# A Mamba and quantised-FFN block on one core: GpSimd's B products in pairs, one C product moved from VectorE to GpSimd

## The chip, the cores and the metric

One core of a Trainium2 chip runs the whole kernel in one launch. The metric is the device time in microseconds (us) from launch to end. A core has TensorE (PE), VectorE (DVE), ScalarE (ACT) and GpSimd (POOL) for computing and SyncE (SP) for issuing most of the transfers; each runs its own instruction stream in order, and they meet at semaphores.

## What is computed

The input x has 8192 tokens of 512 features. First comes a Mamba layer on a modulated layer norm of x, then a feed-forward layer whose inputs and weights are quantised in blocks of 16 to a four-bit grid. Only the Mamba layer's scan is touched by the change. Cut to what matters:

```python
xz = x @ W_in.T;  xc, z = split(xz)             # 1024 inner channels each
xc = silu(conv(xc));  dbc = xc @ W_xproj.T      # delta's rank 32, B and C: 16 states each
delta = softplus(dlt @ W_dt.T + b_dt)
deltaA  = exp(delta[..., None] * A)             # A < 0, one per channel and state
deltaBx = delta[..., None] * B[:, :, None, :] * xc[..., None]
h = deltaA * h + deltaBx                        # along the tokens
y = einsum("bdn,bn->bd", h, C) + xc * D
y = (y * silu(z)) @ W_out.T
```

## The kernel before, in words

**Chunks and units.** The 8192 tokens are cut into 16 chunks of T = 512. Channels lie on the 128 partitions, in eight blocks; two neighbouring blocks make a pair p (four pairs), and each pair has 16 states n. A *unit* u = 16 p + n is one state of one pair: 64 units per chunk. For a unit, tiles are 128 x 2 x 512: two blocks, 512 tokens.

**What happens to a unit.** (1) GpSimd makes the B product (`times_b`, line 717): `slot[u % 8] = du * b_row`, 1024 elements per partition, where du is delta times xc of the pair and b_row is the state's row of B, broadcast to all partitions by a DMA. (2) ScalarE makes the decays exp(rate * delta) in PSUM (`decays`, line 917), two per unit, in two buffers by the parity of u. (3) VectorE scans each of the two blocks (`scan`, line 1050), from the state that the last chunk left. (4) ScalarE saves the last column as the new state (`save_state`, lines 903 and 906). (5) The scan's result is multiplied by c_row. For the 43 units listed in `DVE_C` VectorE does this itself, in two halves right behind the scan (line 1057); for the other 21 (0, 1, 5, 7, 10, 13, 17, 18, 23, 25, 28, 32, 33, 37, 40, 46, 49, 50, 54, 56, 62) GpSimd does it in one instruction (`times_c`, line 724). (6) TensorE adds the unit's product to y by transposing matmuls (`sum_states`, line 1188) and increments `sum_done`, once per unit; that frees the slot.

**Rings.** There are 8 slots, 4 rows of b_row and 4 rows of c_row. A B product of unit u waits for `sum_done` to say that units up to u - 8 are summed, and for its own row of b_row. A load of b_row for unit u waits until B products up to u - 4 are made (`ub_ready`), one of c_row until the C product of u - 4 is made. Each scan of a unit waits for `ub_ready` to reach u + 1.

**The order of the work.** Every engine goes through positions 0 to 63 of each chunk. At position pos GpSimd makes the B product of unit pos, then the C product of unit pos - 2 (`POOL_LAG`) if it is one of its own, then what `POOL_STEPS` lists: a product du at positions 6, 21, 46 and 60, and four tiny operations of the layer norm (`newton`, lines 673 to 676) at 13. VectorE scans unit pos and makes its C product if it is its own; at some positions it adds a gate of the last pair (`DVE_STEPS`, line 963), in the interval after units 4, 5, 21, 32, 36, 49, 51 and 53. TensorE sums unit pos - 3 (`PE_LAG`) and then does what `PE_STEPS` lists: input projections (line 1111), convolution, the small projections, transposes of y and the output projection (lines 1165 and 1169). These tables were written out by hand. At positions 5 to 7 TensorE has the input projections z6 and z7 and five parts of the output projection of the last chunk; z6 needs a PSUM bank that the softplus of pair 1 frees, which ScalarE does at its position 3 (line 853), after the decays of unit 3. Those need the states of unit 1 saved. At its position 15 ScalarE copies a block of the output projection (`residual`, line 872), and TensorE needs that bank before the sum of unit 8. SyncE issues, at each position, the load of b_row for unit pos + 2, the load of c_row for unit pos + 1, and the transfers of `SP_STEPS`.

In chunk 0 the steps that belong to the chunk before are absent, the output projection among them. After the last scan, near 3522 us, the feed-forward layer runs by tiles of 128 tokens.

The GpSimd loop, before:

```python
wait(pool, S["sum_done"], c.at(UNITS, u - SLOTS + 1))
wait(pool, *ring_loaded(b_loaded, c, u))
...
pool.tensor_tensor(slot[:, u % SLOTS, :, :], du[:, p % 2, :, :],
                   two(b_row[:, u % BC_RING, :]), ALU.mult).then_inc(S["ub_ready"], 1)
```

Of the kernel before, what the change touches and what calls it, by code (L numbers as in the profile page):

```python
# [5 lines left out]
P = 128  # L6
# [3 lines left out]
ALU = mybir.AluOpType  # L10
# [5 lines left out]
T = TILES * P  # L16
SLOTS = 8
BC_RING = 4
WIN_RING = 4
UNITS = 64  # L20
# [70 lines left out]
    61: [("load_win", 12, 1)], 63: [("load_win", 13, 1)],  # L91
}
DVE_C = (
    2, 3, 4, 6, 8, 9, 11, 12, 14, 15, 16, 19, 20, 21, 22, 24, 26, 27, 29, 30, 31, 34, 35, 36, 38, 39, 41, 42, 43, 44,
    45, 47, 48, 51, 52, 53, 55, 57, 58, 59, 60, 61, 63,
)

# [21 lines left out]
def wait(eng, sem, value):  # L119
    if not isinstance(value, int) or value > 0:  # L120
        eng.wait_ge(sem, value)
# [9 lines left out]
def adaln_block(nc, x, w_in, w_conv, w_x, w_dt, b_dt, a_log, d_skip, w_out, w_gate, w_up, w_down, c_vec, w_mod, out):  # L131
# [73 lines left out]
    with keep:  # L205
# [3 lines left out]
        def sem(name, stack=keep):  # L209
            return stack.enter_context(nc.semaphore(name))  # L210
# [31 lines left out]
        with mamba:  # L242
            def sb(name, shape, dt=F32, stack=mamba):
                return stack.enter_context(nc.sbuf_tensor(name, shape, dt))
# [20 lines left out]
            du = sb("du", [P, 2, 2, T])  # L265
            slot = sb("slot", [P, SLOTS, 2, T])
            b_row = sb("b_row", [P, BC_RING, T])
# [62 lines left out]
            with setup:  # L330
# [10 lines left out]
                s = lambda name: sem(f"first_{name}", setup)  # L341
# [128 lines left out]
            b_loaded = [sem(f"b_loaded{i}") for i in range(BC_RING)]  # L470
# [14 lines left out]
            S = {n: sem(n) for n in names}  # L485
# [3 lines left out]
            def exists(c):  # L489
                return c.reg is not None or 0 <= c.off < CH  # L490
# [9 lines left out]
            def steps(table, c, pos):  # L500
                return [(step, arg, c.shift(d)) for step, arg, d in table.get(pos, ())
                        if exists(c.shift(d)) and not after_scans(step, c.shift(d)) and not ahead_of_loop(step, c.shift(d))]
# [26 lines left out]
            def two(row):  # L529
                return row.unsqueeze(1).to_broadcast((P, 2, T))  # L530

            def back(c, v):

                return (v, c) if v >= 0 else (v + UNITS, c.shift(-1))
# [10 lines left out]
            def ring_loaded(sems, c, u):  # L545

                per = UNITS // len(sems)
                return sems[u % len(sems)], c.at(16 * per, 16 * (u // len(sems) + 1))
# [6 lines left out]
            with nc.Block() as block:  # L555
# [101 lines left out]
                def _(pool):  # L657
# [26 lines left out]
                    def prep_close(r):  # L684
                        v = prep_rows(r)[:, 0:prep_width(r)]
                        pool.wait_ge(prep_scales, 5 * r + 5)
                        pool.wait_ge(prep_rounded, r + 1)
                        pool.tensor_tensor(blocks(v), blocks(v), spread(prep_scale[r % 3], prep_width(r) // QB),
                                           ALU.mult).then_inc(prep_quant, 1)
                        if r in POOL_SAVES:  # L690
                            prep_save(pool, r)

                    def prepare():
                        for g in range(LAST):
                            prep_mul(g)
                            if g in WOUT_AT:
                                j = 2 * WOUT_AT.index(g)
                                pool.wait_ge(wout_loaded, 16)
                                pool.wait_ge(mix_row, 1)
                                pool.tensor_tensor(wout[:, j:j + 2, :], wout[:, j:j + 2, :],  # L700
                                                   mix_mag.unsqueeze(1).to_broadcast((P, 2, DM)), ALU.mult).then_inc(wout_done, 1)
                            if g >= 1:
                                prep_close(g - 1)
                        prep_mul(LAST)
# [3 lines left out]
                    def times_b(u, c):  # L708
                        p, n = divmod(u, N)
                        if c.reg is None and c.off == 0 and u in range(0, SLOTS, 2):  # L710
                            g = PREP_RING + u // 2
                            pool.wait_ge(prep_saved[g], 16 * len(PREP[g]))
                        wait(pool, S["sum_done"], c.at(UNITS, u - SLOTS + 1))
                        wait(pool, *ring_loaded(b_loaded, c, u))
                        if n == 0:
                            wait(pool, S["u_ready"], c.at(PAIRS, p + 1))
                        pool.tensor_tensor(slot[:, u % SLOTS, :, :], du[:, p % 2, :, :],  # L717
                                           two(b_row[:, u % BC_RING, :]), ALU.mult).then_inc(S["ub_ready"], 1)

                    def times_c(u, c):  # L720
                        h = slot[:, u % SLOTS, :, :]
                        wait(pool, S["state_saved"], c.at(2 * UNITS, 2 * u + 2))
                        wait(pool, *ring_loaded(c_loaded, c, u))
                        pool.tensor_tensor(h, h, two(c_row[:, u % BC_RING, :]), ALU.mult).then_inc(c_row_used[u % BC_RING], 1)  # L724

                    def body(c):
                        for pos in range(UNITS):
                            if exists(c):
                                times_b(pos, c)
                            v, cc = back(c, pos - POOL_LAG)  # L730
                            if exists(cc) and v not in DVE_C:
                                times_c(v, cc)
                            for step, arg, cc in steps(POOL_STEPS, c, pos):
                                HAVE[step](arg, cc)
                                if cc.reg is None and cc.off == 0 and (step, arg) == ("du", 0):
                                    prep_close(LAST - 1)
                            if c.reg is None and c.off == -1 and pos == PREP_AT:
                                prepare()
                            if c.reg is None and c.off == 0 and pos == 3:
                                prep_close(LAST)  # L740
                            if c.reg is None and c.off == CH and pos == PART_ADD_AT:
                                pool.wait_ge(S["part_out"], TILES)
                                for s in range(TILES):
                                    pool.wait_ge(xr_loaded[s], 16 * CH)
                                    pool.tensor_tensor(xr[:, s, :], xr[:, s, :], win[:, s, :, :].rearrange("p k q -> p (k q)"), ALU.add)
                    pool.memset(state[:, :, :], 0.0).then_inc(S["cleared"], 1)
                    pool.memset(halo[:, :, :], 0.0).then_inc(S["cleared"], 1)
                    pool.wait_ge(S["cleared"], 3)
                    all_chunks(pool, body)

                @block.scalar
# [493 lines left out]
        with ffn:  # L1245
# [33 lines left out]
            s = lambda name: sem(name, ffn)  # L1279
# [114 lines left out]
            S = {n: sem("f_" + n, ffn) for n in names}  # L1394
# [475 lines left out]
```

## Time and profile before

| | us |
|---|---|
| three runs | 5140.60, 5141.44, 5143.02 (median 5141.44) |
| profiled execution: span from its first to its last instruction | 5139.8 |
| Mamba half, to the last scan | about 3522 |
| busy in the span: PE / DVE / ACT / POOL | 4759.9 / 4789.5 / 3336.0 / 3832.3 |

The profiled execution has no time of its own beside its span; the span is 1.6 us below the median of the runs. "Busy" is the time in which an engine's records lie. A record of a TensorE matmul ends where it is modelled to end, and records of neighbouring instructions of an engine overlap a little, so spacing (start to start) prices an instruction better than its record. A value in brackets behind a row of the timeline is the idle time of the engine before it and what ended that. L717 is line 717 of the kernel. "x3" in a timeline is three instructions merged in one row.

### The profile page before, as it was taken

The numbers are of one execution on the slowest core, as the hardware profiler recorded it, in microseconds if no ns is written. First come the engines' busy times: TensorE is split into PE (matmuls) and PEld (weight loads), VectorE is DVE, ScalarE is ACT, GpSimd is POOL, SyncE is SP. The second block draws the span as 40 slices with busy tenths as digits, with TensorE's granted clock in tenths as the row PEclk, the third lists the DMA queues.
The fourth block names the chain that finished last, engine by engine and source line by source line (L and its number), as shares of the span: only waits on it lengthen the run. The fifth ranks groups of instructions, "written<-read, shape, count | busy, mean of one in ns | idle before, by whom it ended". The sixth has DMA issues, their size and how long they took to land. (4 is left out here: it accounts for less than half of the span.)

```text
span 5139.8 us, 67238 instructions
## 1 busy us (share of the span) xinstructions
PE 4759.9 (93%) x21964; PEld 3283.1 (64%) x21964; DVE 4789.5 (93%) x5476; ACT 3336.0 (65%) x7037; POOL 3832.3 (75%) x1722
## 2 busy tenths in 40 slices
PE   8799899998999989999999898967999999999999
PEld 3555555555555555555555555555888888888888
DVE  8999999999999999999999999997888888888887
ACT  3777877777777787777777877765444444444442
POOL 6999999999999999999999999994322322322231
PEclk9899999999999999999999999988999999999999
DMA  7555565655656556566566666554010011001000
GB/s 268 173 198 194 189 204 185 196 195 191 199 188 200 195 186 204 186 198 196 188 199 188 194 199 191 187 172 156 25 38 31 31 34 35 31 31 37 31 31 29
DMA packets 402675, 745.79 MB, mean 145 GB/s; under 512 B 44083, under 2 KB 44211, under 8 KB 402198
## 3 DMA queue, kind: packets, MB, share of 16 engines
q1 hardware_dynamic: 401590, 738.08, 43.7%
q8 instruction: 176, 2.88, 0.2%
q0 software_dynamic: 736, 3.41, 0.2%
q14 instruction: 173, 1.42, 0.1%
HBM read 698.05 MB, written 43.26 MB: 144 GB/s over the span
## 5 line engine op out<-in xcount | busy, mean ns | idle before, releaser
L717 POOL TENSOR_TENSOR slot<-du,b_row 128x1024 f32<-128x1024 f32 x1024 | 2397.9, 2379 | 0.2
L1050 DVE TENSOR_TENSOR_SCAN decays<-decays,state,slot 128x512 f32<-128x512 f32 x1376 | 1686.6, 1270 | 61.6 <-POOL slot L717 50.3
L917 ACT ACTIVATE decays<-delta,rate 128x512 f32<-128x512 f32 x2048 | 1385.0, 687 | 50.6 <-DVE slot L998 2.2
L1111 PE MATMUL work_ps<-h_t,win 128*128 128x512 f32 x2048 | 981.8, 627 | 137.5 <-ACT delta L853 109.1
L1188 PEld LDWEIGHTS y_ps<-ident,slot 128*128 128x128 f32 x8192 | 946.2, 143 | 238.2 <-issue 177.9
L1188 PE MATMUL y_ps<-ident,slot 128*128 128x128 f32 x8192 | 1020.9, 277 | 42.6 <-POOL slot L724 30.7
L1574 POOL TENSOR_TENSOR hq<-hid,qinv 128x1408 f32<-128x1408 f32 x63 | 163.5, 2596 | 1001.7 <-DVE qinv L1600 1001.7
L1057 DVE TENSOR_TENSOR slot<-decays,c_row 128x512 f32<-128x512 f32 x1376 | 870.8, 673 | 0.0
L724 POOL TENSOR_TENSOR slot<-slot,c_row 128x1024 f32<-128x1024 f32 x336 | 797.7, 2374 | 81.8 <-ACT state L906 79.7
L1050 DVE TENSOR_TENSOR_SCAN slot<-decays,state,slot 128x512 f32<-128x512 f32 x672 | 819.0, 1263 | 4.0 <-POOL slot L717 2.2
L1111 PEld LDWEIGHTS work_ps<-h_t,win 128*128 128x128 f32 x2048 | 393.7, 201 | 590.0 <-issue 493.1
L1514 ACT ACTIVATE act_gate<-gate_ps 128x512 f32<-128x512 f32 (+1 forms) x192 | 108.3, 564 | 719.9 <-DVE hid L1645 547.5
L1120 PE MATMUL work_ps<-raw,diag 128*128 128x512 f32 x1024 | 465.8, 597 | 27.8 <-ACT raw L798 14.3
L1165 PE MATMUL work_ps<-wout,xc 128*128 128x512 f32 x960 | 447.9, 596 | 32.4 <-ACT xr L872 22.0
L903 ACT ACTIVATE state<-decays 128x1 f32<-128x1 f32 x1376 | 219.1, 159 | 283.7 <-DVE slot L1057 282.6
L1120 PEld LDWEIGHTS work_ps<-raw,diag 128*128 128x128 f32 x1024 | 185.2, 189 | 242.0 <-issue 221.9
L1165 PEld LDWEIGHTS work_ps<-wout,xc 128*128 128x128 f32 x960 | 168.2, 190 | 203.3 <-issue 167.5
L1725 PE MATMUL gate_ps<-w_gate_hi,hx_hi 128*128 128x512 f32 (+1 forms) x768 | 291.9, 380 | 3.4 <-DVE hx_lo L1666 3.4
L1725 PE MATMUL up_ps<-w_up_hi,hx_hi 128*128 128x512 f32 (+1 forms) x768 | 286.0, 372 | 0.0
L1726 PE MATMUL gate_ps<-w_gate_lo,hx_hi 128*128 128x512 f32 (+1 forms) x768 | 286.0, 372 | 0.0
L1727 PE MATMUL up_ps<-w_up_hi,hx_lo 128*128 128x512 f32 (+1 forms) x768 | 285.9, 372 | 0.0
L1727 PE MATMUL gate_ps<-w_gate_hi,hx_lo 128*128 128x512 f32 (+1 forms) x768 | 285.9, 372 | 0.0
(274 smaller groups left out, 7356.9 us busy)
## 6 DMA issues: line engine op xcount, KB each, us to landing
b_row<-b_c_rows SPq DMA_DIRECT2D x1024, 256.0 KB, 3.9
c_row<-b_c_rows SPq DMA_DIRECT2D x1024, 256.0 KB, 3.8
win<-in_w_in SPq DMA_DIRECT2D x256, 256.0 KB, 4.4
xt<-in_x SPq DMA_DIRECT2D x16, 1024.0 KB, 7.1
xr<-in_x SPq DMA_DIRECT2D x64, 256.0 KB, 4.4
x_after_mamba<-xr SPq DMA_DIRECT2D x64, 256.0 KB, 4.6
xa<-x_after_mamba SPq DMA_DIRECT2D x64, 256.0 KB, 3.0
xres<-x_after_mamba SPq DMA_DIRECT2D x64, 256.0 KB, 2.7
```

Of the source, the lines that this page charges most:

```text
L717: pool.tensor_tensor(slot[:, u % SLOTS, :, :], du[:, p % 2, :, :], two(b_row[:, u % BC_RING, :]), ALU.mult).then_inc(S["ub_ready"], 1)
L724: pool.tensor_tensor(h, h, two(c_row[:, u % BC_RING, :]), ALU.mult).then_inc(c_row_used[u % BC_RING], 1)
L917: act.activation(decay[u % 2][:, i, :], delta[:, p % 2, i, :], ACT.Exp, scale=rate[:, 2 * p + i, n:n + 1]).then_inc(S["decay_ready"], 1)
L1050: dve.tensor_tensor_scan(d if u in DVE_C else h, d, h, state[:, 2 * p + i, n:n + 1], ALU.mult, ALU.add).then_inc(S["scan_done"], 1)
L1057: op = dve.tensor_tensor(slot[:, u % SLOTS, i, :], decay[u % 2][:, i, :], c_row[:, u % BC_RING, :], ALU.mult)
L1111: op = pe.matmul(dst[:, :], win[:, i % WIN_RING, k, :], h_t[:, k, :], start=(k == 0), stop=(k == KT - 1))
L1120: op = pe.matmul(dst[:, :], diag[:, j, k, :], raw[:, j % 2, k:k + T], start=(k == 0), stop=(k == TAPS - 1))
L1165: pe.matmul(work_ps[b][:, :], xc[c.parity][:, j, s * P:(s + 1) * P], wout[:, j, :], start=(j == 0), stop=False)
L1188: op = pe.matmul(y_ps[i][:, s, :], slot[:, u % SLOTS, i, s * P:(s + 1) * P], ident[:, :], is_transpose=True, start=False, stop=(n == N - 1 ...
L1725: pe.matmul(dst, lhs[0], rhs[0], start=first, stop=False)
L1726: pe.matmul(dst, lhs[0], rhs[1], start=False, stop=False)
L1727: return pe.matmul(dst, lhs[1], rhs[0], start=False, stop=last)
```

## The change

A B product is made at even units only, for units u and u + 1 in one instruction of 2048 elements per partition. It waits until units up to u - 7 are summed and until both rows of b_row are loaded, and increments `ub_ready` by two when it is done. GpSimd's order becomes: pair (u, u + 1), C product of u - 2, C product of u - 1, pair (u + 2, u + 3), each C product where it is GpSimd's own. Unit 44 leaves the list `DVE_C`, so its C product is GpSimd's. Nothing else is changed; the transfers are the same, with the same waits.

```diff
 DVE_C = (
-    2, 3, 4, 6, 8, 9, 11, 12, 14, 15, 16, 19, 20, 21, 22, 24, 26, 27, 29, 30, 31, 34, 35, 36, 38, 39, 41, 42, 43, 44,
+    2, 3, 4, 6, 8, 9, 11, 12, 14, 15, 16, 19, 20, 21, 22, 24, 26, 27, 29, 30, 31, 34, 35, 36, 38, 39, 41, 42, 43,
     45, 47, 48, 51, 52, 53, 55, 57, 58, 59, 60, 61, 63,
 )
@@ times_b
-                        wait(pool, S["sum_done"], c.at(UNITS, u - SLOTS + 1))
-                        wait(pool, *ring_loaded(b_loaded, c, u))
+                        wait(pool, S["sum_done"], c.at(UNITS, u - SLOTS + 2))
+                        for v in (u, u + 1):
+                            wait(pool, *ring_loaded(b_loaded, c, v))
                         if n == 0:
                             wait(pool, S["u_ready"], c.at(PAIRS, p + 1))
-                        pool.tensor_tensor(slot[:, u % SLOTS, :, :], du[:, p % 2, :, :],
-                                           two(b_row[:, u % BC_RING, :]), ALU.mult).then_inc(S["ub_ready"], 1)
+                        s, r = u % SLOTS, u % BC_RING
+                        pool.tensor_tensor(slot[:, s:s + 2, :, :], du[:, p % 2, :, :].unsqueeze(1).to_broadcast((P, 2, 2, T)),
+                                           b_row[:, r:r + 2, :].unsqueeze(2).to_broadcast((P, 2, 2, T)),
+                                           ALU.mult).then_inc(S["ub_ready"], 2)
@@ body
-                            if exists(c):
+                            if exists(c) and pos % 2 == 0:
                                 times_b(pos, c)
```

## Rows read from the trace of the kernel before

**Rows 1.** The page: engine totals, and busy tenths in 40 slices of the span.

```profile
PE 4759.9 (93%) x21964; PEld 3283.1 (64%) x21964; DVE 4789.5 (93%) x5476; ACT 3336.0 (65%) x7037; POOL 3832.3 (75%) x1722
...
DVE  8999999999999999999999999997888888888887
...
POOL 6999999999999999999999999994322322322231
```

**Rows 2.** One line by its source, L827: count, durations in ns, first and last start.

```profile
L827 ACT ACTIVATE xc<-xc x15: 3621/3624/3640, 300.2 to 3273.7; 128x4096 f32<-128x4096 f32 x15
```

**Rows 3.** The page's groups: count, busy us, mean ns of one, idle before, releaser.

```profile
L717 POOL TENSOR_TENSOR slot<-du,b_row 128x1024 f32<-128x1024 f32 x1024 | 2397.9, 2379 | 0.2
...
L724 POOL TENSOR_TENSOR slot<-slot,c_row 128x1024 f32<-128x1024 f32 x336 | 797.7, 2374 | 81.8 <-ACT state L906 79.7
```

**Rows 4.** The waits: who waited for whom, us in total, times, longest.

```profile
POOL slot L724 <- ACT state L906: 79.7, 83, 5.1
...
DVE decays L1050 <- POOL slot L717: 50.3, 80, 1.0
...
DVE slot L1050 <- POOL slot L717: 2.2, 1, 2.2
```

**Rows 5.** GpSimd's groups by form, other sizes; columns as in rows 3.

```profile
L745 POOL TENSOR_TENSOR xr<-xr,win 128x512 f32<-128x512 f32 x4 | 4.9, 1268 | 0.0
L681 POOL TENSOR_TENSOR zs<-zs,prep_inv 128x2048 f32<-128x2048 f32 x1 | 3.7, 3683 | 0.1
```

**Rows 6.** Timeline of GpSimd, chunk 8, C product 62 to B product 19.

```profile
1822.18 2.35 POOL L724 TENSOR_TENSOR slot<-slot,c_row 128x1024 f32<-128x1024 f32 x1 [1.06 <-ACT state L906]
...
1856.94 6.99 POOL L717 TENSOR_TENSOR slot<-du,b_row 128x1024 f32<-128x1024 f32 x3
...
1876.48 9.32 POOL L717 TENSOR_TENSOR slot<-du,b_row 128x1024 f32<-128x1024 f32 x4
1885.74 2.37 POOL L724 TENSOR_TENSOR slot<-slot,c_row 128x1024 f32<-128x1024 f32 x1
```

**Rows 7.** Timeline of VectorE, chunk 8: units 62, 4, 8, 12, 14, 15, 16, 17, 19.

```profile
1819.35 2.45 DVE L1050 TENSOR_TENSOR_SCAN slot<-decays,state,slot 128x512 f32<-128x512 f32 x2
...
1838.53 2.47 DVE L1050 TENSOR_TENSOR_SCAN decays<-decays,state,slot 128x512 f32<-128x512 f32 x2 [0.98 <-POOL slot L717]
...
1852.46 2.47 DVE L1050 TENSOR_TENSOR_SCAN decays<-decays,state,slot 128x512 f32<-128x512 f32 x2 [0.70 <-POOL slot L717]
...
1865.47 2.46 DVE L1050 TENSOR_TENSOR_SCAN decays<-decays,state,slot 128x512 f32<-128x512 f32 x2
...
1871.98 2.47 DVE L1050 TENSOR_TENSOR_SCAN decays<-decays,state,slot 128x512 f32<-128x512 f32 x2 [0.51 <-POOL slot L717]
...
1875.54 2.46 DVE L1050 TENSOR_TENSOR_SCAN decays<-decays,state,slot 128x512 f32<-128x512 f32 x2
...
1879.09 2.46 DVE L1050 TENSOR_TENSOR_SCAN decays<-decays,state,slot 128x512 f32<-128x512 f32 x2
...
1882.64 4.80 DVE L1050 TENSOR_TENSOR_SCAN slot<-decays,state,slot 128x512 f32<-128x512 f32 x4
1887.36 2.44 DVE L1050 TENSOR_TENSOR_SCAN decays<-decays,state,slot 128x512 f32<-128x512 f32 x2
```

**Rows 8.** Timeline of TensorE, chunk 8, softplus to the sums of units 9 to 12.

```profile
1834.08 6.28 PE L1111 MATMUL work_ps<-h_t,win 128*128 128x512 f32 x8 [4.85 <-ACT delta L853]
...
1863.58 1.91 PE L1188 MATMUL y_ps<-ident,slot 128*128 128x128 f32 x16
...
1875.05 3.66 PE L1188 MATMUL y_ps<-ident,slot 128*128 128x128 f32 x32
```

**Rows 9.** Timeline of ScalarE, chunk 8: softplus and residual(1).

```profile
1832.85 1.08 ACT L853 ACTIVATE delta<-work_ps 128x512 f32<-128x512 f32 x2
...
1872.90 0.57 ACT L872 ACTIVATE xr<-work_ps 128x512 f32<-128x512 f32 x1
```

**Rows 10.** One tile, b_row: its transfers from issue to landing.

```profile
DMA to landing us min/median/max: 3.0/3.9/8.2
```

## The prediction

> **What bounds the kernel now.** I began with the engine totals and the slices [rows 1]. GpSimd (POOL) is at 9 tenths in every slice of the Mamba half and at 2 to 4 afterwards; VectorE (DVE) is at 9 in nearly all of them. The change touches only the first half, which ends near 3522 us; what follows keeps its time.
>
> Next, the length of a chunk. A wide Silu runs once in each of chunks 1 to 15 [rows 2]: (3273.7 - 300.2) / 14 = 212.4 us. Then the costliest groups [rows 3]: per chunk GpSimd makes 64 B products, 21 C products and 4 du; VectorE makes the scans of 64 units and 43 C products. Neighbours overlap a little in the records, so I price by spacing: four B products from 1876.48 to the C product at 1885.74 are 2.315 us each [rows 6]; a unit whose C product is VectorE's takes 3.55 us (1875.54 to 1879.09), one whose C product is GpSimd's takes 2.36 (two in 4.72, 1882.64 to 1887.36) [rows 7]. GpSimd: 89 x 2.315 + 1.0 for four tiny operations = 207.0 us of 212.4. VectorE: 43 x 3.55 + 21 x 2.36 = 202.2, and nine small operations of 0.6 bring it to 207.6. Two engines are equally full, and each waits some 5 us per chunk for the other [rows 4]: the C products 79.7 us (83 times) for a scan, scans 50.3 + 2.2 us for a B product. So the end is set by a chain that crosses between them, not by either sum. The reader should see in rows 3 that no B product waits itself (0.2 us in 1024).
>
> **The change, by sums.** (1) Fewer instructions. The same operation takes 1268 ns for 512 elements [rows 5] and 2374 for 1024 [rows 3]: 2.16 ns an element. 2379 + 1024 x 2.16 = 4.59 us in the record, and 4.53 in spacing (neighbours overlap by 0.06), against 4.63 for two singles: 0.10 saved per pair, 3.2 us per chunk. Bounds for the spacing: 4.69 if three free dimensions cost a start each, 3.62 if it ran like the 2048-element row with one narrow operand, 3683 ns [rows 5]. Nearest is the same operation at two sizes, hence 4.53. The Trainium skill ("GPSIMD Engine Reference", 3.1) gives 4497 ns measured for a 2048-element tensor_tensor; by that the spacing would be 4.43 and the total some 13 us lower. No run here shows it yet. (2) C product 44 moves: VectorE 3.55 - 2.36 = 1.19 us less per chunk, GpSimd 2.315 more. By sums VectorE falls by 1.2 us, GpSimd by 3.2 - 2.3 = 0.9 us, so if every wait stayed, the kernel would gain 16 x 0.9 to 1.2 = 14 to 19 us. Queues: no DMA is added, but loads of b_row are now released two at a time.
>
> **The change, by order.** Three waits change, and they outweigh that.
>
> (a) A scan of an even unit waits for the product of the odd one too: its B product is ready 4.59 - 2.38 = 2.2 us later. The order on GpSimd becomes pair, C(u-2), C(u-1), pair. For an odd unit w whose C product is GpSimd's (1, 5, 7, 13, 17, 23, 25, 33, 37, 49) this closes a loop: scan(w) ends, C(w) starts 0.4 to 0.5 later (the scan of rows 7 that begins at 1819.35 ends at 1821.80, its C product starts at 1822.18 [rows 6]), 2.32 for C(w), 4.59 for pair (w+3, w+4), 0.1 to the scan: 7.4 to 7.5 us until scan(w+3). VectorE has only units w+1 and w+2 to fill it: 7.1 with two of its own C products (0.4 lost), 5.9 with one (1.5 lost), less 0.6 for a gate in between. Before, the loop was 2.2 shorter, and fitted.
>
> (b) The pair needs both slots free, so sum_done to u-7 where a single needed u-8. TensorE (PE) is behind at one place of each chunk. It waits 4.85 us for the softplus [rows 8, 9], then works from 1834.08 without a pause on projections and reaches the sum of unit 5 in the row that starts at 1863.58 (two sums, the first done at 1864.6). B product 12 starts at 1861.56, the third in the x3 row at 1856.94 [rows 6]. As a single it needs the sum of unit 4. In a pair with 13 it needs unit 5's: GpSimd stands still to 1864.7. That point hangs on the softplus, itself behind scan(1), so nothing moves it earlier.
>
> (c) The b_row ring has four rows, so the loads for a pair leave when the pair before the last is done. From issue to landing is 3.9 us in the median [rows 10], issues in a burst start 0.4 apart. About 5.2 us for the last of four against 4.5 for a pair: short by up to 0.7 where no C product lies between, which is so at 11 gaps per chunk. Most of these are where GpSimd is ahead; I count it at nothing and hold it as a rival.
>
> **The walk through one chunk** (rows 6 to 9, chunk 8), as VectorE's waits for slots:
> - Unit 4: C(62), pair, C(0), C(1), pair: the last pair's record ends 3 x 2.315 + 4.53 + 4.59 after 1822.18, at 1838.2, scan(4) follows at 1838.3. Wait 1.0 (before 0.98, and 0.3 at unit 3).
> - Unit 8: C(5) at scan(5) + 0.45, then pair (8, 9): scan(8) as before, wait 0.8 (0.70).
> - Unit 12: 1864.7 + 4.59 + 0.1 = 1869.4 against 1865.47: wait 3.9 (none).
> - Unit 14: GpSimd is free at 1869.2, C(10) to 1871.5, the tiny four to 1872.5, pair (14, 15): scan at 1877.2. VectorE is ready at 1869.4 + 3.55 + 2.36 = 1875.3: wait 1.9 (0.51).
> - Unit 16: the sum of unit 9 lies behind residual(1), which ScalarE (ACT) runs behind scan(13); it moves by the 3.9 from 1876.1 (the first of four sums in the row at 1875.05) to 1880.0 [rows 8, 9]. Pair (16, 17) gives scan 16 at 1884.8 (1880.1 + 4.59 + 0.1), VectorE is ready at 1884.3: 0.5.
> - Unit 20: loop of 17, units 18 and 19 hold 5.9: 1.5. Unit 22: C(18), du and the pair make it ready 2 x 2.315 + 4.53 = 9.2 after scan 20 is, VectorE needs 2 x 3.55 + 0.6 = 7.7: 1.5. Unit 26: loop of 23: 1.5.
> - From 27: loops of 25, 33, 37 and 49 at 0.2 to 0.4 each, and the sum that the pair (62, 63) needs: 1.2.
>
> Together 13.8 us. Before it was (50.3 + 2.2) / 16 = 3.3 [rows 4]. So a chunk grows by 13.8 - 3.3 - 1.2 = 9.3 us: 140 us for 15 chunks, and about 3 for chunk 0, where TensorE has no output projection and (b) is absent. **+143 us.** The profiled span is 5139.8 us, the median of the three runs 5141.4, 1.6 above it. 5139.8 + 1.6 + 143 = 5284. Slack of GpSimd (waits in its C products) is lost or grows; it shortens nothing.
>
> **Rivals.**
> - R1, the sum is not late: only the loops of (a) cost. Units 12 and 14 then hold 0.3, 16 nothing: 13.8 - 6.3 + 0.3 = 7.8; 7.8 - 3.3 - 1.2 = 3.3 us, x16 = 53: **5194**. For it: TensorE could catch up with a softplus that comes earlier. Against: that softplus follows scan(1), which does not move.
> - R2, the sums rule, faster: VectorE's 19 us are gained, **5122**. It needs every even-unit product to be 2.2 us early. It decides at the scan of unit 20: if that starts within 5.9 us of the end of scan 17. Rows 7 show waits of 0.5 to 1.0 at even units 4, 8 and 14 already, so there is no such lead in the first half of a chunk.
> - R3, the loads of (c) or a spacing of 4.69 come on top: 11 x 0.7 = 7.7 us with half of it on the path, or 0.16 at each of the 8 paired waits (1.3 us): 1.3 to 7.7 us per chunk more, 20 to 120; with 5.4 it is 86: **5370**.
> - R4, the long instruction runs at 3.62: 0.9 less at eight waits, 9.3 - 7.2 = 2.1 us, **5175**.
> - R5, the two effects cancel, within 0.2%: it needs waits of 4.5 us per chunk in place of 13.8.
>
> **How the numbers follow.** Forecast 0.57 (its own range 5240 to 5320, the waits at units 12 to 16 being the softest), R1 0.19, R3 0.12, R4 0.03, R2 0.06, R5 0.03. The likeliest gives 5284. Range 5180 to 5350: it leaves out R2, R5, R4 and most of R3. A measurement of this kernel can tell about 0.2% (10 us) from no change. Slower by more than that: 0.91; within: 0.03; faster: 0.06.
>
> **What the profile after would show.** L717 512 times at about 4590 ns; GpSimd's sum a little lower, while its share in the Mamba slices drops below 9 tenths. The scans' idle time before them, released by POOL slot L717, near 220 us, in few long waits of 1 to 4 us. L717 itself idle before it some 60 to 90 us, released by the sums (PE y_ps L1188): that is (b). A chunk of 221 to 222 us by the Silu row. With the chunk at 215 and L717 not waiting for PE, R1 was right. L717 idle behind DMA of b_row shows R3. A chunk below 212 and fewer scan waits prove the walk wrong, and with it the view that order outweighs the sums.

## The result and the profile after

The changed kernel takes 5402.6 us in the median of four runs, the kernel before 5141.0 beside it: a ratio of 1.051, 95% interval 1.049 to 1.052. It is 261.6 us slower. I had forecast 143 us more and a range up to 5350; the direction was right, the size fell outside the range.

The page of the changed kernel: engine totals, busy tenths, and the groups that answer to [rows 1] and [rows 3] (out<-in, count | busy us, mean ns | idle before, what ended most of it).

```profile
PE 4836.9 (90%) x21964; PEld 3332.0 (62%) x21964; DVE 4781.6 (89%) x5444; ACT 3341.2 (62%) x7021; POOL 3798.8 (70%) x1226
...
DVE  8899898998989889898898989889688888888888
...
POOL 6989898988989889998898989888222222232321
...
L719 POOL TENSOR_TENSOR slot<-du,b_row 128x2048 f32<-128x2048 f32 x512 | 2317.3, 4534 | 267.5 <-PE y_ps L1191 139.0
L1053 DVE TENSOR_TENSOR_SCAN decays<-decays,state,slot 128x512 f32<-128x512 f32 x1344 | 1650.3, 1273 | 326.2 <-POOL slot L719 294.0
...
L727 POOL TENSOR_TENSOR slot<-slot,c_row 128x1024 f32<-128x1024 f32 x352 | 828.7, 2358 | 110.9 <-ACT state L909 110.4
```

Both engines have less to do than before, GpSimd by 33.5 us and VectorE by 7.9, and both stand still more. In the Mamba slices GpSimd is down from 9 tenths to 8 in about every second slice; I had forecast a share below 9. The B products, which never waited (0.2 us, [rows 3]), now wait 267.5 us.

The waits of the changed kernel, against [rows 4] (us in total, times, longest):

```profile
DVE decays L1053 <- POOL slot L719: 294.0, 177, 5.2
...
POOL slot L719 <- PE y_ps L1191: 139.0, 43, 5.4
...
POOL slot L719 <- DMA b_row<-b_c_rows: 124.3, 110, 3.4
...
DVE decays L1053 <- ACT decays L920: 31.2, 27, 1.7
...
DVE slot L1053 <- POOL slot L719: 14.9, 38, 4.4
```

The sum closes. By the profile's attribution the scans wait 294.0 + 14.9 - 50.3 - 2.2 = 256.4 us more for B products and some 19 more for decays (31.2 against 12); the C product that went to GpSimd takes 16 x 1.19 = 19 off VectorE. That leaves 256 of the 261.7 us between the two spans (5401.5 and 5139.8). So the scans' waits are the loss. The same line by its source gives the length of a chunk, against [rows 2]:

```profile
L830 ACT ACTIVATE xc<-xc x15: 3620/3625/3632, 308.3 to 3520.8; 128x4096 f32<-128x4096 f32 x15
```

(3520.8 - 308.3) / 14 = 229.5 us in place of 212.4.

Where in a chunk the waits lie: VectorE's timeline of the changed kernel, chunk 8, cut to rows in which it waited, units 4, 8, 12, 14, 16, 20, 22, 26, 36, 48 and 58. They answer to [rows 7].

```profile
1965.98 2.47 DVE L1053 TENSOR_TENSOR_SCAN decays<-decays,state,slot 128x512 f32<-128x512 f32 x2 [1.89 <-POOL slot L719]
...
1979.91 2.47 DVE L1053 TENSOR_TENSOR_SCAN decays<-decays,state,slot 128x512 f32<-128x512 f32 x2 [0.83 <-POOL slot L719]
...
1996.66 2.47 DVE L1053 TENSOR_TENSOR_SCAN decays<-decays,state,slot 128x512 f32<-128x512 f32 x2 [3.66 <-POOL slot L719]
...
2004.42 2.47 DVE L1053 TENSOR_TENSOR_SCAN decays<-decays,state,slot 128x512 f32<-128x512 f32 x2 [1.75 <-POOL slot L719]
...
2014.23 2.47 DVE L1053 TENSOR_TENSOR_SCAN decays<-decays,state,slot 128x512 f32<-128x512 f32 x2 [2.62 <-POOL slot L719]
...
2027.56 2.47 DVE L1053 TENSOR_TENSOR_SCAN decays<-decays,state,slot 128x512 f32<-128x512 f32 x2 [1.44 <-POOL slot L719]
...
2036.71 2.47 DVE L1053 TENSOR_TENSOR_SCAN decays<-decays,state,slot 128x512 f32<-128x512 f32 x2 [1.36 <-ACT decays L920]
...
2050.06 2.47 DVE L1053 TENSOR_TENSOR_SCAN decays<-decays,state,slot 128x512 f32<-128x512 f32 x2 [1.44 <-POOL slot L719]
...
2083.89 2.47 DVE L1053 TENSOR_TENSOR_SCAN decays<-decays,state,slot 128x512 f32<-128x512 f32 x2 [1.24 <-ACT decays L920]
...
2124.88 2.47 DVE L1053 TENSOR_TENSOR_SCAN decays<-decays,state,slot 128x512 f32<-128x512 f32 x2 [2.13 <-POOL slot L719]
...
2160.35 2.47 DVE L1053 TENSOR_TENSOR_SCAN decays<-decays,state,slot 128x512 f32<-128x512 f32 x2 [1.27 <-POOL slot L719]
```

Every row shown is at an even unit; no odd unit waits 0.1 us or more in the mean. At units 22 and 36 the bracket names the decays, yet that is not what held the scan: in the mean of chunks 2 to 14 the first decays were ready 0.94 and 3.07 us before VectorE was free, the B product 1.26 us after it, at both units. Set against the walk (means of the bracketed times over chunks 2 to 14):

| unit | forecast | measured |
|---|---|---|
| 2 and 4 | 1.0 | 0.67 + 1.90 |
| 8 | 0.8 | 0.91 |
| 12 | 3.9 | 3.59 |
| 14 | 1.9 | 1.76 |
| 16 | 0.5 | 2.57 |
| 20, 22, 26 | 1.5 each | 1.44, 1.39, 1.43 |
| from 27 on | 1.2 | 5.8, of which 36: 1.39, 48: 2.48, 58: 0.77 |
| sum | 13.8 | 21.5 |

GpSimd's timeline around units 12 to 17 of the same chunk shows how unit 16 came to that:

```profile
1992.03 4.52 POOL L719 TENSOR_TENSOR slot<-du,b_row 128x2048 f32<-128x2048 f32 x1 [5.43 <-PE y_ps L1191]
...
1999.81 4.50 POOL L719 TENSOR_TENSOR slot<-du,b_row 128x2048 f32<-128x2048 f32 x1
2004.27 2.36 POOL L727 TENSOR_TENSOR slot<-slot,c_row 128x1024 f32<-128x1024 f32 x1
2009.56 9.03 POOL L719 TENSOR_TENSOR slot<-du,b_row 128x2048 f32<-128x2048 f32 x2 [2.93 <-PE y_ps L1191]
```

Pair (12, 13) stands 5.43 us until the sum of unit 5 is made: the place is the one of the walk. Pair (16, 17) stands another 2.93 us for the sum of unit 9. TensorE's timeline and the stretches (busy us of PE, PEld, DVE, ACT, POOL with counts; then the granted clock, DMA share, GB/s) tell why that sum is late. The first two blocks are the changed kernel, the last two the kernel before:

```profile
2004.82 0.77 PE L1138 MATMUL work_ps<-dt_parts,wdt 98*128 98x512 f32 x1 [5.16 <-ACT xr L875]
2005.38 1.91 PE L1191 MATMUL y_ps<-ident,slot 128*128 128x128 f32 x8
```

```profile
1999.00:2004.00 5.00, 0.66 (x2) 0.00 (x0) 3.67 (x5) 3.62 (x8) 4.76 (x5) 0.91 0.54 189
2004.00:2010.00 6.00, 5.18 (x22) 4.86 (x23) 5.58 (x6) 3.67 (x8) 3.07 (x3) 0.50 0.80 286
```

```profile
1873.62 0.47 PE L1135 MATMUL work_ps<-dt_parts,wdt 98*128 98x512 f32 x1 [1.25 <-ACT xr L872]
```

```profile
1873.00:1876.00 3.00, 2.38 (x19) 2.26 (x20) 3.00 (x5) 2.03 (x5) 3.00 (x2) 1.00 0.60 193
```

Behind the 3.7 us that VectorE lost at unit 12, ScalarE's residual(1) is late, TensorE has nothing to do for 5.16 us, and then it runs at a granted clock of 0.50, the 1.2 GHz level. The Trainium skill ("TensorE: Matmul & The Clock Gate", Part 1) says that an idle TensorE falls to the lower clock; the trace agrees here, with 0.50 behind 5.16 us of idling. In the kernel before, the same matmuls came behind 1.25 us of idling and ran at 1.00. From the start of residual(1) to the end of the sum of unit 9 it took 5.3 us (2004.10 to 2009.42) against 3.2 before (1872.90 to 1876.08). TensorE starts 0.72 us behind the start of residual(1) in both kernels, so the whole difference lies in the matmuls: 4.60 us (2004.82 to 2009.42) against 2.46 (1873.62 to 1876.08).

### The profile page after: what moved, and what is told of

Its sections match the earlier page's. It is cut to its first block and busy times, and to the rows that moved or that the text cites. A ratio compares the mean times of both kernels' runs of the same rounds, so it can differ in the third digit from the quotient of the medians.

```text
span 5401.5 us, 66714 instructions
## 1 busy us (share of the span) xinstructions
PE 4836.9 (90%) x21964; PEld 3332.0 (62%) x21964; DVE 4781.6 (89%) x5444; ACT 3341.2 (62%) x7021; POOL 3798.8 (70%) x1226
## 5 line engine op out<-in xcount | busy, mean ns | idle before, releaser
L719 POOL TENSOR_TENSOR slot<-du,b_row 128x2048 f32<-128x2048 f32 x512 | 2317.3, 4534 | 267.5 <-PE y_ps L1191 139.0
L1053 DVE TENSOR_TENSOR_SCAN decays<-decays,state,slot 128x512 f32<-128x512 f32 x1344 | 1650.3, 1273 | 326.2 <-POOL slot L719 294.0
L1191 PEld LDWEIGHTS y_ps<-ident,slot 128*128 128x128 f32 x8192 | 981.5, 147 | 285.3 <-issue 174.2
L1191 PE MATMUL y_ps<-ident,slot 128*128 128x128 f32 x8192 | 1062.5, 283 | 79.6 <-POOL slot L727 39.6
L727 POOL TENSOR_TENSOR slot<-slot,c_row 128x1024 f32<-128x1024 f32 x352 | 828.7, 2358 | 110.9 <-ACT state L909 110.4
L1053 DVE TENSOR_TENSOR_SCAN slot<-decays,state,slot 128x512 f32<-128x512 f32 x704 | 859.0, 1265 | 15.4 <-POOL slot L719 14.9
L1060 DVE TENSOR_TENSOR slot<-decays,c_row 128x512 f32<-128x512 f32 x1344 | 852.0, 675 | 0.0
L1123 PE MATMUL work_ps<-raw,diag 128*128 128x512 f32 x1024 | 480.9, 614 | 53.6 <-DVE xc L966 30.1
```

The lines of the kernel that those rows point to most:

```text
L719: pool.tensor_tensor(slot[:, s:s + 2, :, :], du[:, p % 2, :, :].unsqueeze(1).to_broadcast((P, 2, 2, T)), b_row[:, r:r + 2, :].unsqueeze(2) ...
L1053: dve.tensor_tensor_scan(d if u in DVE_C else h, d, h, state[:, 2 * p + i, n:n + 1], ALU.mult, ALU.add).then_inc(S["scan_done"], 1)
L1060: op = dve.tensor_tensor(slot[:, u % SLOTS, i, :], decay[u % 2][:, i, :], c_row[:, u % BC_RING, :], ALU.mult)
L1123: op = pe.matmul(dst[:, :], diag[:, j, k, :], raw[:, j % 2, k:k + T], start=(k == 0), stop=(k == TAPS - 1))
L1191: op = pe.matmul(y_ps[i][:, s, :], slot[:, u % SLOTS, i, s * P:(s + 1) * P], ident[:, :], is_transpose=True, start=False, stop=(n == N - 1 ...
```

## The experiments

My theory after this reading was the forecast's own, with more weight on (c): an even unit's late signal (a), two slots needed at once (b), two rows of b_row needed at once (c). The rivals were the long instruction itself, the moved C product, and the later place of the C products. Where a run has a ratio with an interval, it was measured six to ten times. The six from "Only the pairs" to "Both remedies" are a single execution each; four of the changed kernel spread over 6 us, so their differences of 10 us or less say little.

**Only the C product of unit 44 moves.** The list `DVE_C` as in the change, B products single as before.

```diff
-    ..., 39, 41, 42, 43, 44,
+    ..., 39, 41, 42, 43,
```

> Only the C product of unit 44 is GpSimd's; B products are single as before. Theory (the loss comes from the order and the grain of the B products): VectorE is relieved of 1.2 us per chunk in the stretch where GpSimd waited for it (4.8 us per chunk), so 5122 to 5146 us, scans' waits for slots 2.5 to 5 us per chunk. Rival (the moved product overfills GpSimd and is a large part of the 261 us): 5180 or more.

5158.8 us, ratio 1.0034 (1.0022 to 1.0047): 18 us slower, 13 us above the band of the theory and 21 below the rival. The waits of this run:

```profile
DVE decays L1059 <- POOL slot L726: 84.0, 110, 1.7
```

They were 50.3. The new ones are at units 47 and 53 (1.6 and 0.7 us, means as above). GpSimd's timeline, chunk 8:

```profile
1978.81 2.35 POOL L726 TENSOR_TENSOR slot<-du,b_row 128x1024 f32<-128x1024 f32 x1
1982.37 2.36 POOL L733 TENSOR_TENSOR slot<-slot,c_row 128x1024 f32<-128x1024 f32 x1 [1.21 <-ACT state L915]
1984.68 2.37 POOL L665 TENSOR_TENSOR du<-delta,xc 128x1024 f32<-128x1024 f32 x1
1987.00 4.69 POOL L726 TENSOR_TENSOR slot<-du,b_row 128x1024 f32<-128x1024 f32 x2
```

C product 44 comes while GpSimd is ahead, so it first waits 1.2 us for its scan, then takes 2.3, and a du stands behind it before B product 47. Here GpSimd's idle time was no room for work that has itself to wait for VectorE. So the half of the change that the sums priced as a gain is a loss on its own.

**Only the pairs.** The change without its edit to `DVE_C`.

> Pairs, but the C product of unit 44 stays on VectorE. Theory: 5385 to 5420 us, the same places of waiting as the changed kernel. Rival (the moved product is a large part): 5360 or less.

5368.0 us: between the two expectations. The places of waiting are those of the changed kernel, but for unit 48, where the 2.5 us are gone. The pairs cost 227 us, the moved product 18 alone and 35 on top of them. Unit 48 shows why it costs more there (means over chunks 2 to 14). In the kernel before, its B product was ready 4.4 us before VectorE was free for its scan. With the moved product alone 1.35 us of that lead are left, with the pairs alone 1.05; with both, the product comes 2.35 us late. Each cost fits into the lead by itself, and both together do not.

**Singles in the pairs' order.** At an even position both B products are made, each by its own instruction, with its own waits and signal. C product 44 is GpSimd's, here and in all runs down to "Pairs only where GpSimd leads".

```diff
-                            if exists(c):
+                            if exists(c) and pos % 2 == 0:
                                 times_b(pos, c)
+                                times_b(pos + 1, c)
```

> GpSimd's order of the changed kernel (B of u, B of u+1, C of u-2, C of u-1), but two instructions of 1024 elements, each with its own wait for its slot and its b_row and its own signal. Theory (what costs is that an even unit is signalled with the odd one, and that both slots and both rows are needed at the start): most of the loss is gone, 5140 to 5190 us. Rival (the C products' later place costs): above 5300.

5162.1 us, as the theory had it, and within 4 us of the run that moves the C product alone. In the sum the C products' later place costs next to nothing. It isn't nothing everywhere: the scans at units 3 to 8 wait 1.0 us where they waited 2.0, the one at 14 waits 1.9 where it waited 0.5.

**The same, and the scan of an even unit waits for the odd one's product.**

```diff
-                            wait(dve, S["ub_ready"], c.at(UNITS, u + 1))
+                            wait(dve, S["ub_ready"], c.at(UNITS, u - u % 2 + 2))
```

> As the run before with singles in pair order, but the scan of an even unit also waits for the odd unit's B product. This brings back the late signal alone, without the slots and rows needed together and without the long instruction. Theory: waits of 1.4 us at units 20, 22 and 26, some 1 us at 4, 8 and 14, none of 3.6 at 12; 8 to 9 us per chunk, 5185 to 5250 us. Rival (the late signal is the whole loss): near 5400. Rival (the long instruction itself slows the others): below 5170.

5292.1 us: the late signal alone costs 130 us over the run before, half of the whole loss, and the time lies 42 us above my band. VectorE's timeline of chunk 8, units 20, 22 and 26:

```profile
1971.91 2.47 DVE L1060 TENSOR_TENSOR_SCAN decays<-decays,state,slot 128x512 f32<-128x512 f32 x2 [1.58 <-POOL slot L726]
...
1981.22 2.46 DVE L1060 TENSOR_TENSOR_SCAN decays<-decays,state,slot 128x512 f32<-128x512 f32 x2 [1.52 <-POOL slot L726]
...
1994.70 2.47 DVE L1060 TENSOR_TENSOR_SCAN decays<-decays,state,slot 128x512 f32<-128x512 f32 x2 [1.58 <-POOL slot L726]
```

These are the loops of (a) near the forecast size, with no long instruction in the program (means 1.6, 1.1 and 1.6 us); unit 12 now waits 1.3 in place of 3.6. The expectation was too low at units 4 and 14 (1.55 and 1.9 us for about 1), and it had nothing at 12 and nothing from unit 27 on, where this run waits 3.7 us per chunk, 1.25 of it at 36 and 1.1 at 48. The run before waits 1.0 there, so the late signal makes 2.7 us of waiting in that part of a chunk, where the prediction had 1.2 for everything.

**Single B products at 12, 13, 16 and 17, pairs elsewhere.** `PAIRED` holds the even units but 12 and 16; a single waits as before the change.

```diff
+                        w = 2 if u in PAIRED else 1
-                        wait(pool, S["sum_done"], c.at(UNITS, u - SLOTS + 2))
-                        for v in (u, u + 1):
+                        wait(pool, S["sum_done"], c.at(UNITS, u - SLOTS + w))
+                        for v in range(u, u + w):
```

> Changed kernel, but units 12, 13, 16 and 17 have single B products. Theory (GpSimd's waits for the sums at 12 and 16 reach VectorE): the scans' waits at units 12 and 16 (3.6 and 2.6 us) go, the one at 14 falls to about 0.5: 5 to 7 us per chunk, 5290 to 5325 us. Rival (GpSimd has slack that only moves the wait): 5380 or more, with longer waits at units 14 and 20.

5318.4 us, 84 less than the changed kernel. The waits at 12 and 16 are gone (3.6 and 2.6); the one at 14 grows from 1.8 to 2.9 where I expected 0.5. The trace of this run says why (chunk 8; GpSimd, then TensorE, then the stretch of TensorE's work with its clock):

```profile
1960.10 4.53 POOL L722 TENSOR_TENSOR slot<-du,b_row 128x2048 f32<-128x2048 f32 x1 [1.69 <-PE y_ps L1197]
```

```profile
1963.94 0.47 PE L1144 MATMUL work_ps<-dt_parts,wdt 98*128 98x512 f32 x1 [1.40 <-ACT xr L881]
```

```profile
1963.00:1967.00 4.00, 3.06 (x25) 2.94 (x26) 2.27 (x2) 1.50 (x3) 4.00 (x3) 1.00 0.22 56
```

GpSimd now comes to pair (14, 15) earlier and stands 1.69 us there, for the sum of unit 7: (b) has moved to the next pair. GpSimd's wait for sums falls from 139.0 to 28.3 us, and 23.6 of these are at that pair. TensorE's stall ahead of the sum of unit 8 is down to 1.40 us, its clock stays at 1.00, and the same matmuls up to the sum of unit 9 take 2.46 us again (1963.94 to 1966.40). So (b) at units 12 and 16, with the slow clock that follows from it, is worth 5.6 us per chunk, less what it moves to 14. That includes the early signals that singles give back at these two units; by the run with the late signal alone, up to 1.3 us of it is that.

**The rows of b_row ahead of those of c_row** in SyncE's queue, pairs everywhere.

```diff
-                            v, cc = forth(c, pos + 2)
-                            if exists(cc):
-                                load_b(v, cc)
+                            for d in (3, 4) if pos % 2 else ():
+                                v, cc = forth(c, pos + d)
+                                if exists(cc):
+                                    load_b(v, cc)
```

> Changed kernel, but SyncE issues both loads of b_row of a pair together, at the odd position three before it, ahead of the c_row load that waits for a C product. Theory (the rows land late because they stand behind c_row and other loads in SyncE's queue): GpSimd's waits for b_row fall from 124 us to under 30, the scans' waits at units 4, 36, 48 and 58 fall by 4 to 5 us per chunk: 5320 to 5350 us. Rival (they are late since the ring has only four rows): 5380 or more.

5355.6 us, 47 less, just outside the band. The waits of this run:

```profile
POOL slot L720 <- PE y_ps L1192: 92.5, 22, 5.4
POOL slot L720 <- issue: 71.2, 31, 3.9
...
POOL slot L720 <- DMA b_row<-b_c_rows: 9.3, 3, 3.1
```

For b_row it is 9.3 us in place of 124.3. Of the 71.2 whose releaser the profile does not name, 44.8 are at pair (16, 17), where the changed kernel waited 44.3 for the sums; 13.0 and 13.5 are at pairs 58 and 62 and may still be b_row. The scans' waits at units 48 and 58 vanish and 0.9 us comes back at 47 behind the decays; those at 4 and 36, which I expected to fall too, hardly do (1.9 to 1.7, 1.4 to 1.1). What stood in the way can be read in SyncE's timeline of the changed kernel, before pair (46, 47):

```profile
2104.55 0.32 SPq L610 DMA_DIRECT2D c_row<-b_c_rows  x1
2104.92 0.43 SPq L585 DMA_DIRECT2D win<-in_w_in  x1
2105.39 0.43 SPq L601 DMA_DIRECT2D b_row<-b_c_rows  x1
2105.87 0.43 SPq L610 DMA_DIRECT2D c_row<-b_c_rows  x1
2106.34 0.43 SPq L601 DMA_DIRECT2D b_row<-b_c_rows  x1
```

The first c_row load waits for C product 40, which GpSimd ends at 2104.49; the row of unit 47 is the fourth load behind it, and lands 4.4 us after its issue, at 2110.7. Pair (44, 45) is done at 2109.0.

**Both remedies.**

> Both edits together: single B products at 12, 13, 16, 17, and b_row loads ahead. Theory (the causes add up): 5402 less 80 to 110 less 50 to 80, so 5215 to 5270 us; what is left is the late signal of even units. Rival (they cover each other): above 5290.

5277.1 us: 125.5 less, where the two alone give 84.2 + 47.1 = 131. They nearly add up. It lies 7 us over my band, since the second gave less than expected. What is left is mostly (a), and (b) at pair (14, 15), where GpSimd still stands 1.7 us. The kernel is 15 us below the one with the late signal alone (5292).

**Pairs only where GpSimd leads**, at 0 and 44 to 62, and the moved C product.

> Unit 44's C product on GpSimd, pairs only at units 0 and 44 to 62, where the B product was ready 2 us or more before its scan. Theory: no new wait of VectorE beyond a few tenths, so 5115 to 5150 us. Rival (b_row loads and the sums cost there too, units 46 to 58 had 2.4, 1.0 and 1.6 us of waiting for b_row): 5170 to 5220.

5154.3 us, ratio 1.0026 (1.0015 to 1.0036); between the bands. Its scans wait 1.4 us at unit 48 and 0.8 at 58. At 58 that is the row of b_row (GpSimd stands 1.5 us there), as in the changed kernel. At 48 it is not: GpSimd waited 0.1 us for b_row at pair (46, 47), and C product 44 and the du stand in front as in the first run. But units 3 to 14 wait 1.4 us in place of 2.5. That was new, and I took it apart.

**One pair, at units 0 and 1**, nothing else changed from the kernel before.

> The kernel before with one pair per chunk, at units 0 and 1, and nothing else. In the run with pairs at 0 and 44 to 62 the scans' waits at units 3, 4, 8 and 14 had fallen from 3.0 to 1.4 us (means of chunks 2 to 14: 0.31 to 0.98 each before) and GpSimd's wait in C product 62 from 1.1 to none. Theory (GpSimd does B product 1 in the time in which it stood waiting for scan 62, and reaches the full stretch 1 us earlier): 1 us per chunk, 5120 to 5132 us. Rival (the gain came from the other pairs): 5138 to 5145.

5130.6 us, ratio 0.9980 (0.9971 to 0.9989): 10 us faster, by the theory. GpSimd made product 1 where it had stood 1.06 us before C product 62 ([rows 6], first row). The scans' waits for slots are down from 52.5 to 23.6 us, a part comes back as waits for decays (21.3 in place of 10.9):

```profile
DVE decays L1059 <- ACT decays L926: 21.3, 32, 5.2
DVE decays L1059 <- POOL slot L726: 19.2, 35, 0.7
```

**The same order with two single instructions.**

```diff
-                            if exists(c):
+                            if exists(c) and pos != 1:
                                 times_b(pos, c)
+                                if pos == 0:
+                                    times_b(1, c)
```

> As the run before, but B products 0 and 1 are two instructions, both ahead of C product 62. Theory (the gain is the order, not the longer instruction, which is worth 0.1 us): 5120 to 5135 us, within 3 us of the run before. Rival (the pair's length matters): 5138 or more.

5130.7 us, ratio 0.9981 (0.9971 to 0.9991), the same as with the pair. The gain is the order.

**The pair at 0, C product 44 moved, and the du of pair 3 at position 44 in place of 46**, ahead of C product 44.

> Pair at 0, C product 44 on GpSimd, and the product du of pair 3 made at position 44 in place of 46, ahead of the C product that waits 1.2 us for scan 44. With the C product alone moved VectorE waited 1.6 us at unit 47 and 0.7 at unit 53, behind that wait and the du. Theory (the moved product pays where GpSimd's idle time is really filled): both waits fall under 0.4, VectorE keeps the 1.2 us: another 10 to 19 us less than with the pair at 0 alone, 5103 to 5120 us. Rival (GpSimd has no room for 2.3 us more in that stretch): 5125 or more.

5130.4 us, ratio 0.9979 (0.9970 to 0.9989): no better than the pair alone, a miss. Units 47 and 53 wait 0.3 and 0.65 us, which eats most of the 1.19 that VectorE is relieved of. The rival's band was right: even so the moved product gains nothing.

**Also a pair at 6**, added to the run before.

> As the run before with a pair at units 6 and 7 too, where the B product was ready 2.7 us before its scan. Theory: 0.1 us saved on GpSimd in its full stretch, so 0 to 3 us less. Rival (the pair is late by its b_row, which stands behind the c_row load for C product 1): up to 20 us more.

5126.3 us, ratio 0.9973 (0.9962 to 0.9984), the fastest of all. Six of its seven times (5125.98 to 5127.73) lie below all ten of the run before (5127.95 to 5131.44), but the intervals overlap: that the second pair helps is likely and not shown. It is 14 us faster than the kernel before.

## Why the prediction was right in direction and wrong in size

**Right.** The price of the long instruction: 4534 ns in the record and 4.49 us in spacing (median of 86 that follow one another without a gap), for 4.59 and 4.53 forecast. A pair saves 0.14 us, for 0.10 forecast. The Trainium skill ("GPSIMD Engine Reference", 3.1) has 4497, closer in the record. "By order" over "by sums": GpSimd has 33.5 us less to do, and the kernel is 261.6 us slower. The loops of (a) came out within 0.1 us at units 20, 22 and 26, the stall of (b) within 0.3 at units 12 and 14.

The runs can be set in a row: the moved product and the order 21 us (5162.1 - 5141.0), then the late signal 130, then from that run to "Both remedies" 15 less (5292.1 - 5277.1), and what "Both remedies" takes away, (c) and (b) at units 12 and 16, 125.5 on top. These steps sum to 261.6 us by construction, since each starts where the last ends; what is shown is the size of each step, in this order. The 15 us are fewer instructions and what else differs between those two runs, and are not taken apart.

**The size.** The walk had 13.8 us of waiting per chunk, and it was 21.5. The 7.7 missing make 116 us in 15 chunks, and 143 + 116 is 259 of the 261.6. They lie at three places: 4.6 from unit 27 on, 2.1 at unit 16 and 1.6 at units 2 and 4; the others are 0.6 less than forecast.

**Wrong: the term "From 27: 1.2", which measured 5.8**, and with it "Most of these are where GpSimd is ahead; I count it at nothing" for (c). I did not walk through that half unit by unit. In the kernel before, the B product was ready ahead of VectorE by 2.9 us at unit 34, 4.4 at 48 and 2.6 at 58, but by only 0.26 at 36. Three costs drew on that lead. The late signal takes 2.2 us at every even unit; added to the singles in the pairs' order it raises the waiting from 27 on from 1.0 to 3.7 us. The late rows take 2.0 and 2.4 at pairs 34 and 46, where I had priced the burst at 0.7: I had counted four loads and not those of `SP_STEPS` in between, and the load in front of the burst itself waits for a GpSimd C product. With all loads moved ahead, the 5.8 fall to 3.15. The moved product takes 3.1 at unit 48; without it they fall to 2.9. The gains of the last two overlap, since either alone empties the wait at 48 (2.48 us). The sums had the moved product as a gain of 1.2 us on VectorE; it cost 18 us alone and 35 on top of the pairs.

**Wrong: unit 16 at 0.5 us, measured 2.57.** The step shifted the sum of unit 9 rigidly with scan 13. It took no account of TensorE's clock, which after 5.16 idle us was half: 2.1 us more for the same matmuls. The first stall had a second price here.

**Wrong: the start of the walk, units 2 and 4 at 1.0 together, measured 2.57.** I took C product 62 from the kernel before, 0.4 us behind its scan. In the changed kernel it stands behind pair (0, 1) and started 1.3 us behind the scan (chunk 8: the scan ends at 1948.36, the C product starts at 1949.67), and everything behind it is later by that.

**Wrong: the chance of the rivals.** R3 was the case nearest to what happened, and I gave it 0.12, with "half of it on the path". Its price, 20 to 120 us on top, held the 118.6 that were missing, but not for its reason: the rows were worth 47. R1 (5194), R2 (5122), R4 and R5 fell.

Left open: how the late rows, the moved product and the late signal share the waits from unit 27 on, since they overlap; and what the stall would have cost at the full clock, since no run had the 5.16 us of idling without the lower clock behind it.

## What to carry to other kernels

Where two engines are both full and wait for each other, an instruction that is merged saves its start (here 0.14 us) but delays the first half's signal by the second half's length (2.2 us), and it needs both halves' buffers and inputs at its own start. Price those two before the start, unit by unit, from how early each half was ready in the trace, and add up everything that draws on the same lead: two costs that each fit into it can overrun it together. Idle time of an engine is room only for work that is already ready: one B product made ahead of a C product that waits gave 10 us, one more C product in idle time of the same kind cost 18.

## What was unexpected of the hardware

TensorE at the lower clock of 0.50 (1.2 GHz) right behind a stall of 5.16 us that another engine's wait had caused, where the same work had run at 1.00 behind stalls of 1.25 and 1.40 us: 8 transposing matmuls in 1.91 us against 1.04. A load of b_row took the same 3.9 us from issue to landing in the median in both kernels; the rows were late by their place in SyncE's queue, not by slower transfers: issued ahead, they took 3.6 us, and GpSimd's wait for them fell from 124.3 to 9.3 us.
